# A message-passing layer on one core: sums over gathered slots at two of every three routed groups, with new instruction orders

## The reference

```python
h = x @ W_in2f
Wij = ssp(f_ij @ W_filt1 + b_filt1) @ W_filt2 + b_filt2
Wij = Wij * rcut_ij[:, None]
x_ij = h[idx_j] * Wij
agg = jax.ops.segment_sum(x_ij, idx_i, num_segments=n_atoms)
out = ssp(agg @ W_out1 + b_out1) @ W_out2 + b_out2
```

## Time and profile before

| | us |
|---|---|
| median of three runs | 2133.01 (2132.39 to 2133.57) |
| time of the profiled execution | 2138.0 |
| its span from first to last instruction | 2136.2 |
| PE busy | 2010.7 (94%) |
| DVE busy | 1957.4 (92%) |
| POOL busy | 1695.9 (79%) |
| ACT busy | 1586.3 (74%) |

### The profile page before, as it was taken

The page is one execution under the profiler, slowest core; times in us unless marked ns, Lnnn a source line. Parts: engine busy times, 40 slices in busy tenths (PEclk is TensorE's granted clock), DMA queues, the critical chain, the costliest instruction groups (busy, mean ns, idle before and its releaser), DMA issues.

```text
span 2136.2 us, 53343 instructions
## 1 busy us (share of the span) xinstructions
PE 2010.7 (94%) x16433; PEld 1700.0 (80%) x16433; DVE 1957.4 (92%) x4022; ACT 1586.3 (74%) x3852; POOL 1695.9 (79%) x1051
## 2 busy tenths in 40 slices
PE   2589999999999999999999999999999999999946
PEld 2478888888888888888888888888888888888723
DVE  5579999999999999999999999999999999999837
ACT  1278788788787787887887878778878878778517
POOL 2358888888888888888888888888888888888854
PEclk8789999999999999999999999999999999999979
DMA  8546666665666566666666665666666666655574
GB/s 321 224 91 99 105 96 96 102 103 98 99 98 104 90 99 104 100 94 104 99 99 97 98 104 92 97 103 100 96 102 100 98 98 98 103 90 84 97 196 128
DMA packets 346340, 235.27 MB, mean 110 GB/s; under 512 B 86087, under 2 KB 325554, under 8 KB 345850
## 3 DMA queue, kind: packets, MB, share of 16 engines
q0 software_dynamic: 140976, 64.22, 32.6%
q1 hardware_dynamic: 194598, 150.79, 26.8%
q10 hardware_dynamic: 10476, 16.77, 2.1%
...
...
## 4 chain that ended last, share of the span: by engine, by line
PE 65%; DMA 13%; POOL 7%; issue 7%; DVE 4%; ACT 2%; SPq 1%; POOLq 0%; DVEq 0%; ACTq 0%
PE unit_psum L1739 18%; PE unit_psum L1759 15%; PE both_psum L1695 12%; DMA table<-total,index 11%; PE total_psum L1708 8%; POOL table L789 7%; PE pre_psum L1676 6%; PE both_psum L1720 4%; PE both_psum L1691 2%; DMA x_t<-in_x_t 1%; DMA src_g<-in_src 1%; ACT out_rows L1083 1%; DVE route_hot L1377 1%; DVE scat_hot L1391 0%; DVE acc_t L1406 0%
## 5 line engine op out<-in xcount | busy, mean ns | idle before, releaser
L789 POOL DMA_INDIRECT table<-total,index x979 | 1614.7, 1649 | 334.3 <-issue 237.6
L1739 PE MATMUL unit_psum<-moving,route_hot 128*128 128x258 f32 x4088 | 637.3, 295 | 3.1 <-DVE acc_t L1406 2.1
L1739 PEld LDWEIGHTS unit_psum<-moving,route_hot 128*128 128x128 f32 x4088 | 526.2, 190 | 48.7 <-ACT ring L961 32.7
L1391 DVE TENSOR_SCALAR scat_hot<-node_iota,ring 128x448 fp32r<-128x448 uint16 x1022 | 479.7, 482 | 17.5 <-PE unit_psum L1759 13.1
L939 ACT ACTIVATE h_dst<-both_psum,edge_cols 128x128 f32<-128x128 f32 x1564 | 446.1, 379 | 49.0 <-PE both_psum L1720 48.6
L961 ACT ACTIVATE ring<-unit_psum 128x258 fp32r<-128x258 f32 x1022 | 370.5, 403 | 150.1 <-PE unit_psum L1739 136.2
L1759 PE MATMUL unit_psum<-scat_hot,ring 64*128 64x448 f32 x4088 | 461.1, 372 | 11.2 <-DVE acc_t L1406 9.7
L1759 PEld LDWEIGHTS unit_psum<-scat_hot,ring 64*128 64x128 f32 x4088 | 377.4, 186 | 88.1 <-ACT ring L961 37.8
L1695 PE MATMUL both_psum<-w_f,hidden 128*128 128x128 f32 x3128 | 422.1, 278 | 0.0
L1377 DVE TENSOR_SCALAR route_hot<-node_iota,slot_cols 128x896 fp32r<-128x896 uint16 x584 | 403.9, 725 | 1.8 <-PE unit_psum L1739 1.6
L1695 PEld LDWEIGHTS both_psum<-w_f,hidden 128*128 128x128 f32 x3128 | 398.5, 192 | 5.5
...
## 6 DMA issues: line engine op xcount, KB each, us to landing
dst_b<-dst SPq DMA_DIRECT2D x391, 128.0 KB, 3.3
...
table<-total,index POOLq DMA_INDIRECT x979
...
window<-h_parts SPq DMA_DIRECT2D x391, 32.0 KB, 2.0
...
```

The lines of the kernel that those rows point to most:

```text
L789: pool.indirect_dma_start(tables[k], bass.IndirectOffsetOnAxis(index[:, i, k:k + 1], 0), total[:, i, k, 0:DIM], None, compute_op=ALU.add). ...
L1391: dve.tensor_scalar(scat_hot[:, (n - 1) % HOTS, :], node_iota[:, 0:BUCKET], ring[:, RING_AT[r[1], slot_tile(s)], 2 * DIM:2 * DIM + 1].bitc ...
L1739: last = pe.matmul(unit_psum[:, k % 2, 0:MOVING], route_hot[:, tile, k * P:(k + 1) * P], moving[:, tile, :], start=(tile == 0), stop=(tile ...
```

## The change

`ROUTED_AT` becomes `(2, 4, 7)` and `STEPS_AT` `(0, 2)`: two steps for three routed groups, so that each step takes ten or eleven of them. That makes 104 steps and 44 places in the ring. Each routed tile is summed once, as before. All four written orders, `unit` and `rest`, are new. Below stand the constants, DVE's and PE's `unit`, and the end of PE's `rest`; ACT's and SP's have the same calls in another order, with `copy_total` of the groups 5 and 6 of a period played at the start of the next.

```diff
@@ -15,12 +15,12 @@
 QUAD = 4
 UNIT = 20
 PERIOD = 8
-ROUTED_AT = (1, 4, 6)
+ROUTED_AT = (2, 4, 7)
 LAST_PERIOD = 384
-LAST_ROUTED = (385, 388)
+LAST_ROUTED = (386, 388)
 ROUTE_GROUPS = tuple(g for g in range(LAST_PERIOD) if g % PERIOD in ROUTED_AT) + LAST_ROUTED
 ROUTES = len(ROUTE_GROUPS)
-STEPS_AT = (0, 1, 2)
+STEPS_AT = (0, 2)
 UNITS = -(-GROUPS // UNIT)
 SLOTS = UNITS * UNIT
 QUADS = SLOTS // QUAD
@@ -666,27 +666,26 @@
                 def g(n): return plus(u, n)
...
@@ -1410,136 +1410,137 @@
                 def pair(n): return (u[0], u[1] // 2 + n)
                 def s(n): return (u[0], u[1] // PERIOD * len(STEPS_AT) + n)
                 def r(n): return (u[0], u[1] // PERIOD * len(ROUTED_AT) + n)
-                slot_one_hot(s(-2), 6)
+                mark_repeated(g(-3), plain)
+                make_index(g(-3), plain)
                 multiply(g(0), plain)
+                route_one_hot(r(-1), 0); route_one_hot(r(-1), 1); route_one_hot(r(-1), 2)
                 split_lo(r(-1))
-                route_one_hot(r(-1), 2); route_one_hot(r(-1), 3)
-                slot_one_hot(s(-1), 0)
-                add_slice(s(-2), 0)
-                mark_repeated(g(-1), plain)
-                make_index(g(-1), plain)
-                add_slice(s(-2), 1)
-                slot_one_hot(s(-1), 1)
+                route_one_hot(r(-1), 3)
+                compare_dst(g(3))
+                mark_repeated(g(-2), plain)
                 multiply(g(1), plain)
-                slot_one_hot(s(-1), 2)
-                compare_src(g(3), plain)
                 compare_dst(g(4))
-                slot_one_hot(s(-1), 3)
+                make_index(g(-2), plain)
                 compare_dst(g(5))
                 mark_repeated(g(0), plain)
                 multiply(g(2), plain)
-                slot_one_hot(s(-1), 4)
+                finish_hidden(pair(2))
                 make_index(g(0), plain)
-                finish_hidden(pair(2))
-                slot_one_hot(s(-1), 5)
                 route_one_hot(r(0), 0); route_one_hot(r(0), 1)
-                slot_one_hot(s(-1), 6)
-                route_one_hot(r(0), 2); route_one_hot(r(0), 3)
                 split_lo(r(0))
-                mark_repeated(g(2), plain)
+                route_one_hot(r(0), 2)
+                slot_one_hot(s(-1), 7); slot_one_hot(s(-1), 8)
+                compare_dst(g(6))
+                slot_one_hot(s(-1), 9); slot_one_hot(s(-1), 10)
+                multiply(g(3), plain)
+                route_one_hot(r(0), 3)
+                slot_one_hot(s(0), 0); slot_one_hot(s(0), 1)
                 add_slice(s(-1), 0); add_slice(s(-1), 1)
-                make_index(g(2), plain)
-                multiply(g(3), plain)
-                compare_dst(g(6))
-                slot_one_hot(s(0), 0); slot_one_hot(s(0), 1)
-                compare_dst(g(7))
-                slot_one_hot(s(0), 2); slot_one_hot(s(0), 3)
+                mark_repeated(g(1), plain)
+                slot_one_hot(s(0), 2)
                 multiply(g(4), plain)
                 finish_hidden(pair(3))
+                slot_one_hot(s(0), 3)
+                compare_dst(g(7))
                 slot_one_hot(s(0), 4)
-                compare_src(g(5), plain)
+                compare_src(g(5), plain); compare_src(g(6), plain)
+                make_index(g(1), plain)
+                compare_src(g(8), plain)
+                mark_repeated(g(3), plain)
+                slot_one_hot(s(0), 5)
                 compare_dst(g(8))
-                slot_one_hot(s(0), 5)
+                multiply(g(5), plain)
+                slot_one_hot(s(0), 6)
                 route_one_hot(r(1), 0); route_one_hot(r(1), 1)
-                mark_repeated(g(3), plain)
-                slot_one_hot(s(0), 6)
+                make_index(g(3), plain)
+                multiply(g(6), plain)
                 route_one_hot(r(1), 2)
-                slot_one_hot(s(1), 0)
-                make_index(g(3), plain)
-                multiply(g(5), plain)
-                slot_one_hot(s(1), 1)
+                slot_one_hot(s(0), 7); slot_one_hot(s(0), 8); slot_one_hot(s(0), 9)
+                finish_hidden(pair(4))
+                slot_one_hot(s(1), 0); slot_one_hot(s(1), 1)
                 route_one_hot(r(1), 3)
                 split_lo(r(1))
                 add_slice(s(0), 0); add_slice(s(0), 1)
-                multiply(g(6), plain)
                 compare_dst(g(9))
-                finish_hidden(pair(4))
-                slot_one_hot(s(1), 2); slot_one_hot(s(1), 3)
-                mark_repeated(g(5), plain)
+                slot_one_hot(s(1), 2)
+                compare_src(g(9), plain)
                 compare_dst(g(10))
-                compare_src(g(7), plain); compare_src(g(8), plain)
-                slot_one_hot(s(1), 4)
-                make_index(g(5), plain)
-                compare_src(g(10), plain)
+                compare_src(g(11), plain)
+                slot_one_hot(s(1), 3)
                 multiply(g(7), plain)
-                slot_one_hot(s(1), 5)
-                route_one_hot(r(2), 0); route_one_hot(r(2), 1)
-                compare_dst(g(11))
+                slot_one_hot(s(1), 4); slot_one_hot(s(1), 5)
                 finish_hidden(pair(5))
+                slot_one_hot(s(1), 6)
 
...
@@ -1767,96 +1768,95 @@
                 def pair(n): return (u[0], u[1] // 2 + n)
                 def s(n): return (u[0], u[1] // PERIOD * len(STEPS_AT) + n)
                 def r(n): return (u[0], u[1] // PERIOD * len(ROUTED_AT) + n)
-                sum_slots(s(-2), 1); sum_slots(s(-2), 2); sum_slots(s(-2), 3); sum_slots(s(-2), 4)
-                sum_slots(s(-2), 5); sum_slots(s(-2), 6)
+                route(r(-2), 5); route(r(-2), 6)
+                sum_repeated(g(-2), plain)
                 first_layer(pair(2))
                 gather(g(2))
                 second_layer(g(1))
+                sum_repeated(g(0), plain)
                 route(r(-1), 0)
-                sum_repeated(g(0), plain)
+                gather(g(3))
                 route(r(-1), 1); route(r(-1), 2)
-                gather(g(3))
                 second_layer(g(2))
                 route(r(-1), 3); route(r(-1), 4)
-                sum_repeated(g(2), plain)
+                sum_repeated(g(1), plain)
                 route(r(-1), 5); route(r(-1), 6)
                 first_layer(pair(3))
-                sum_slots(s(-1), 0); sum_slots(s(-1), 1); sum_slots(s(-1), 2); sum_slots(s(-1), 3)
-                sum_slots(s(-1), 4); sum_slots(s(-1), 5); sum_slots(s(-1), 6)
                 gather(g(4))
                 second_layer(g(3))
-                route(r(0), 0); route(r(0), 1)
+                sum_slots(s(-1), 0); sum_slots(s(-1), 1); sum_slots(s(-1), 2); sum_slots(s(-1), 3)
+                sum_slots(s(-1), 4); sum_slots(s(-1), 5); sum_slots(s(-1), 6); sum_slots(s(-1), 7)
+                sum_slots(s(-1), 8); sum_slots(s(-1), 9); sum_slots(s(-1), 10)
                 gather(g(5))
                 second_layer(g(4))
-                route(r(0), 2); route(r(0), 3)
+                route(r(0), 0)
                 sum_repeated(g(3), plain)
-                route(r(0), 4)
+                route(r(0), 1); route(r(0), 2)
+                first_layer(pair(4))
                 gather(g(6))
+                route(r(0), 3); route(r(0), 4)
+                second_layer(g(5))
                 route(r(0), 5); route(r(0), 6)
-                first_layer(pair(4))
                 gather(g(7))
-                second_layer(g(5))
+                second_layer(g(6))
                 sum_slots(s(0), 0); sum_slots(s(0), 1); sum_slots(s(0), 2); sum_slots(s(0), 3)
-                sum_slots(s(0), 4); sum_slots(s(0), 5); sum_slots(s(0), 6)
-                second_layer(g(6))
-                route(r(1), 0)
-                sum_repeated(g(5), plain)
-                route(r(1), 1); route(r(1), 2)
+                sum_slots(s(0), 4); sum_slots(s(0), 5); sum_slots(s(0), 6); sum_slots(s(0), 7)
+                sum_slots(s(0), 8); sum_slots(s(0), 9)
                 gather(g(8))
                 first_layer(pair(5))
-                route(r(1), 3); route(r(1), 4)
+                sum_repeated(g(5), plain)
+                route(r(1), 0); route(r(1), 1)
                 second_layer(g(7))
-                route(r(1), 5); route(r(1), 6)
+                route(r(1), 2); route(r(1), 3)
                 gather(g(9))
+                route(r(1), 4)
                 second_layer(g(8))
-                sum_repeated(g(7), plain)
-                sum_slots(s(1), 0)
 
             def rest():
-                sum_slots((0, 142), 1); sum_slots((0, 142), 2); sum_slots((0, 142), 3); sum_slots((0, 142), 4)
-                sum_slots((0, 142), 5); sum_slots((0, 142), 6)
...
                 second_layer((0, 390))
-                route((0, 145), 0); route((0, 145), 1)
-                sum_repeated((0, 389), plain)
-                route((0, 145), 2); route((0, 145), 3); route((0, 145), 4)
```

(20 more changed lines are left out.)

237 lines of the change are left out of this document (122 added, 115 removed).

## The result

The changed kernel takes **2140.97 us** in the median of six runs (2139.61 to 2143.27), the kernel before 2132.70 (2132.26 to 2133.83): a ratio of 1.0035, with an interval of 1.0024 to 1.0047. It is slower by a third of a per cent. The forecast was 2113, faster by nine tenths of a per cent.

The account below looks back on a forecast made before the run. POOL's scatters were taken to bound the kernel, with PE close behind. From the profiled 2138.0 us, 22 off for DVE's new order and 2 added at the end gave 2118; the median stands 5 lower: 2113 us, range 2089 to 2140.

Parts of the forecast that it names:

- What bounds the kernel: Middle stage: POOL's scatters set the period of 39.0 us; PE is the next bound at 37.8 us.
- rival D: All of the 1.07 us a period of scatter excess goes and PE keeps up: 2084 us, chance 0.10.
- (1): Fewer `acc_t` adds, 304 to 208, take 51 us off DVE, hidden by POOL's queue: 0 in the sum.
- (2): PE around the slot blocks: fewer turns of `unit_psum` save PE 0.25 us a period, behind POOL: 0 in the sum.
- (3): DVE's new order shortens the longest compare sequences, so scatter excess falls 0.45 us a period: 22 us off.
- The two old places: DVE's two longest unbroken compare sequences, 3.3 and 3.1 us, where long scatters stood: 1.07 of 2.2 us excess a period.
- the compares hit as often wherever they stand: Rival B: POOL keeps its 39.0 us a period, only the end's 0 to 4 us remain: 2135, chance 0.15.
- (4): Other groups routed, indices at uneven times: POOL still finds work and does not starve, 0 us.
- The sign that I named for it: POOL waiting for indices or totals for more than 10 us in the stage would show the no-starvation step wrong.
- (5): SP's loads in another order and ACT's later copies of totals run ahead of POOL: 0 us.
- (6): After the last route tile PE has 37 sums left instead of 28: +2 us, between 0 and +4.
- Rival C: Slower: one more long scatter each period, 18 us, and 4 at the end: 2155; mean scatter over 1655 ns; chance 0.20.

Follow-up runs that it names:

- b_half: The kernel before with each scatter of 64 rows instead of 128: 2124.64 us, ratio 0.9936.
- b_nohot: The kernel before with all `route_hot` and `scat_hot` compares cut to 8 columns: 2124.03 us, ratio 0.9933.
- a_half: The changed kernel with each scatter of 64 rows instead of 128: 2114.01 us, ratio 0.9886.
- b_thin: The kernel before with the two `acc_t` adds of every third step cut to 8 of 448 columns: 2129.09 us, ratio 0.9982.
- a_pe: The changed kernel with some 6 of 21 slot sums a period on PE at 64 columns instead of 448: 2138.46 us, ratio 1.0020.
- a_pe_swap: The changed kernel with part of PE's slot sums at 64 columns, and one `route_hot` and `moving` swapped on DVE: 2124.88 us, ratio 0.9941.
- a_swap: The changed kernel in full with one `route_hot` and `moving` swapped in DVE's order: 2144.87 us, ratio 1.0037.
- b_swap1: The kernel before with one `scat_hot` a period put behind group 3's index and group 5's message on DVE: 2133.50 us, ratio 0.9987.
- a_thin: The changed kernel with the `acc_t` adds of every second step cut to 8 of 448 columns: 2133.89 us, ratio 0.9997.
- `a_` kernels: The changed kernel with one experimental edit or another; times differ by run.
- `b_` kernels: The kernel before with one experimental edit or another; times differ by run.

## Why the prediction was wrong, by its steps

**What bounds the kernel.** That POOL sets the pace of the kernel before, with 0.30 us and its excess, was right, but only just. That PE needs only 37.8 us was not: b_half and b_nohot put it at 39.0. I had added up undisturbed pieces and left out the hand-overs between them. The room under the 39.14 us of the kernel before was 0.14 us, not 1.2. In the new order it is larger, since a_half reaches 38.70, but the 1.07 us a period of rival D could not be had. The Trainium skill ("Perfetto Trace Analysis", Identifying the Most-Contended Engine) would judge by the weight loads, 1497 of 1750 us in b_nohot; by that PE had 14% of room, and the measured period says it had next to none.

**(1) The adds: 0.** Right for the kernel before: b_thin, with some 46 us less on DVE, gains 4. What the 51 us would be worth beneath POOL stays open.

**(2) PE's waits: 0 in the sum.** The term was right as far as it went: the weight loads' waits for the ring are gone, and with POOL relieved the new order is 0.30 us a period faster on PE (a_half against b_half), where I had 0.25. In the changed kernel itself it didn't turn into room: PE stands idle for 13 us of the stage, and its weight loads wait 34.1 us for `pick`.

**(3) The new order: -22 us.** This step failed in its size and its reason. Measured is an excess down by 8.6 us over the kernel, 0.18 us a period, where I took 0.45; and the profiled execution of the kernel before stands 5 us above its median, so even the 8.6 are uncertain by some 5. I had seen the two places with the longest scatters, seen the longest sequences of compares beside them, and taken the length for the cause. What the excess follows is the contact: which instruction runs when a scatter begins, for how long it has, and which come next. That is shown by an experiment for one contact (a_pe against a_pe_swap, with a_swap as the control) and by the agreement of the groups for the rest; b_swap1 did not bear it out. The two old places of 0.31 and 0.30 us in the mean went, as I said, but twelve of the new order's twenty positions now pay 0.07 to 0.27 us each, where eleven of the old one's paid 0.07 or more. The order of DVE alone does not set which contacts happen; the phase does so too, and that comes out of the time of all engines. I put the chance of "the compares hit as often wherever they stand" at 0.15; it was nearest to what happened to the excess.

**(4) No starvation: 0.** This is the other step that failed, and the larger miss: the gaps rose by 16.6 us, 12 of them in the stage ahead of a scatter whose index came 0.86 us before it, and 2.7 at the end. I compared the gap between indices (13 us) with POOL's work per group, by DVE's order alone, and left out when DVE can start on that order. Group 5's marking and index stand behind the most crowded 11 us of DVE, which start only when PE has come through its slot sums. By the prediction 0.4 us once a period would eat the whole gain; it was 0.25. The sign that I named for it, 10 us of waits for indices, stands nowhere: the profile books 1.2 us under the index and the rest under "issue". Only the constant 0.86 us from index to scatter shows it. What would have closed the gap at no cost stays open: three attempts to make the index sooner made it worse, and a_thin and a_pe closed it at the price of more excess.

**(5) Other queues: 0.** In the steady periods nothing speaks against it. The first scatter is 2.9 us later, but it stands between 122.1 and 126.2 us in the `a_` kernels and between 120.8 and 124.2 in the `b_` kernels, so most of this is spread between executions. The buffers fill in one jolt; which edit of SP's or ACT's order brings this was not tried.

**(6) The end: +2.** From the last route copy to the load of `parts` it takes 28.0 us (2027.83 to 2055.86), where 30 to 34 were expected and the kernel before took 30.2. In other profiled executions the way from that copy to the last add varies by up to 2 us with the same sums left, so the sign is open; nine more sums cost no more than that.

**The sum.** For +5.3 us instead of -20: (3) gave 8.6 instead of 22, (4) cost 16.6 instead of 0, the start 2.9, and the stretch behind the last scatter is 5.4 shorter. Rival C had the right side with the wrong mechanism: the mean scatter was 1641 ns, not over 1655. The rule of the Trainium skill that I weighed ("SBUF — State Buffer", Who interferes with whom: a VectorE instruction with at most one SBUF input, outside the two-port modes, leaves GpSimd alone) bore out for the adds of the kernel before, 24 ns in the mean over 87 scatters; in the changed kernel it is 57 ns over 54, with what follows an add inside the same scatter's time.
